# Second attention: ScalarE's copies of minus the maxima also for five odd full tiles of each head

## The reference

```python
x = x + attn_a(layernorm(x))      # 16 heads of 64, full softmax, own norm behind it
x = x + ffn(layernorm(x))         # 128 -> 512 -> 128, relu
x = x + attn_b(layernorm(x))      # 8 heads of 128, rope, causal
x = x + ffn(layernorm(x))

def attn_b(x):                    # called the second attention below
    q, k, v = x @ w_aq, x @ w_ak, x @ w_av          # per head, 128 wide
    q, k = rope(q), rope(k)
    s = einsum('ihd,jhd->hij', q, k) / 128
    s = s - 1e30 * (i < j)                          # causal
    p = softmax(s)
    return (p @ v) @ w_ao
```

## Time and profile before

| what | value |
|---|---|
| median of 3 runs | 1911.57 us (1911.49 to 1912.69) |
| the profiled execution, its own time | 1914.15 us |
| span of its profile | 1912.3 us |
| PE busy in the span | 1838.2 us (96%) |
| ACT busy | 1620.6 us (84%) |
| POOL busy | 1596.8 us (84%) |
| DVE busy | 1458.4 us (76%) |
| exponentials of even tiles, copies L938 | 160 |
| seeds L942 | 159 |

### The profile page before, as it was taken

One profiled execution on the slowest core, in us unless ns is written; L12 is line 12 of the kernel. 1 busy time (PEld: TensorE's weight loads), 2 busy tenths in 40 slices (PEclk: granted clock), 3 DMA queues, 4 the chain that ended last, 5 costly groups with the idle time before them and its releaser, 6 DMA issues.

```text
span 1912.3 us, 56624 instructions
## 1 busy us (share of the span) xinstructions
PE 1838.2 (96%) x23763; PEld 1259.8 (66%) x23763; DVE 1458.4 (76%) x2679; ACT 1620.6 (85%) x2080; POOL 1596.8 (84%) x1022
## 2 busy tenths in 40 slices
PE   4899999999999999999999999779999999999998
PEld 3566666666666666666666666447777777777766
DVE  7798878878878878878878875567777778777752
ACT  4799999999999999999999999648787787887884
POOL 2899999999999999999999999448787787887852
PEclk8999999999999999999999999789999999999999
DMA  4201101100100100100100100100000000000000
GB/s 117 67 11 27 35 12 25 35 13 24 35 15 22 35 17 21 35 16 22 35 19 19 35 2 2 56 1 2 2 2 2 2 2 2 2 2 2 2 2 23
DMA packets 45038, 38.01 MB, mean 20 GB/s; under 512 B 8304, under 2 KB 44144, under 8 KB 44528
## 3 DMA queue, kind: packets, MB, share of 16 engines
q1 hardware_dynamic: 44544, 34.19, 7.1%
q10 hardware_dynamic: 240, 0.20, 0.0%
HBM read 8.15 MB, written 1.05 MB: 5 GB/s over the span
## 4 chain that ended last, share of the span: by engine, by line
PE 78%; POOL 8%; DVE 5%; issue 5%; ACT 4%; DMA 0%; SPq 0%; POOLq 0%; ACTq 0%; DVEq 0%
PE ST L1684 11%; PE ST L1685 11%; PE RING L1555 7%; PE OO L1646 6%; PE OO L1648 6%; PE OO L1645 6%; POOL PBUF L711 6%; PE OO L1555 4%; PE ST L1749 2%; PE ST L1882 2%; PE OO L1770 2%; PE ST L1884 1%; PE ST L1883 1%; PE OO L1904 1%; PE OO L1906 1%
## 5 line engine op out<-in xcount | busy, mean ns | idle before, releaser
L627 POOL TENSOR_TENSOR PAB<-PR,PAB 128x1024 f16<-128x1024 f32 x342 | 724.2, 2133 | 42.1 <-ACT PAB L814 40.1
L814 ACT ACTIVATE PAB<-ST,exp_scale 128x1024 f16<-128x1024 f32 x512 | 569.1, 1112 | 0.0
L1139 DVE TENSOR_REDUCE maxes<-RING 128x1 f32<-128x512 f32 x661 | 440.3, 685 | 122.6 <-PE RING L1555 118.1
L1645 PE MATMUL OO<-VP,PAB 128*128 128x66 f16 x4096 | 446.6, 192 | 2.9 <-POOL PAB L627 2.9
L1646 PE MATMUL OO<-VP,PAB 128*128 128x64 f16 x4096 | 447.1, 193 | 0.0
L1648 PE MATMUL OO<-VP,PAB 128*128 128x66 f16 x4096 | 445.2, 192 | 0.0
L812 ACT ACTIVATE PR<-ST,exp_scale 128x1024 f32<-128x1024 f32 x342 | 382.7, 1119 | 66.3 <-PE ST L1685 64.1
L1645 PEld LDWEIGHTS OO<-VP,PAB 128*128 128x128 f16 x4096 | 380.3, 96 | 78.3 <-issue 15.6
L1646 PEld LDWEIGHTS OO<-VP,PAB 128*128 128x128 f16 x4096 | 377.0, 97 | 60.7
L1684 PE MATMUL ST<-QL,KH 128*128 128x512 f16 x1024 | 389.1, 380 | 2.1 <-DVE QH L1151 1.0
L1685 PE MATMUL ST<-QH,KL 128*128 128x512 f16 x1024 | 389.1, 380 | 0.0
(11 more groups left out here) (320 smaller groups left out, 4159.3 us busy)
## 6 DMA issues: line engine op xcount, KB each, us to landing
KH<-HS SPq DMA_DIRECT2D x126, 64.0 KB, 2.0
QL<-HS SPq DMA_DIRECT2D x64, 64.0 KB, 2.0
QL<-LS SPq DMA_DIRECT2D x64, 64.0 KB, 2.0
QH<-HS SPq DMA_DIRECT2D x64, 64.0 KB, 2.0
KL<-LS SPq DMA_DIRECT2D x63, 64.0 KB, 2.0
X<-in_L_attn_a_x SPq DMA_DIRECT2D x4, 256.0 KB, 3.9
SHARED<-in_rope_cos SPq DMA_DIRECT2D x1, 1024.0 KB, 4.9
SHARED<-in_rope_sin SPq DMA_DIRECT2D x1, 1024.0 KB, 7.3
```

Of the source, the lines that this page charges most:

```text
L627: pool.tensor_tensor(PB[:, s, :], PRA[g % PR_SLOTS], PA[:, s, :], ALU.subtract).then_inc(p_low_ready, 1)
L814: act.activation(PA[:, step % SLOTS_A, :], ST[step % 2][:, :], ACT.Exp, scale=scale).then_inc(sa.exps, 1)
L1139: dve.reduce_max(maxes[:, i // BLOCKS, i % BLOCKS:i % BLOCKS + 1], bank[:, :], X_AXIS).then_inc(sa.ring_taken, 1)
L1645: pe.matmul(o, high, v[:, 0:V2_AT], start=(m == 0 and qt == 0), stop=False, skip_group_check=True)
```

## The change

The table `SEEDED_TOO` names five places of a head: (2, 3), (2, 7), (3, 3), (3, 7) and (3, 11). All are odd and full tiles. `seeded(t)` is true for every even tile but 0, as before, and for these. For a seeded tile t, ACT treats tile t - 2 as it treated even tiles before: one exponential from the bank, the high part as a copy from SBUF, and then the seed of tile t. PE leaves out the four spread matmuls of t and waits for the seed. The semaphores `first_exps` and `seeds` now count by `SEEDED_COUNT`. The five tiles of t - 2 are (2, 1), (2, 5), (3, 1), (3, 5) and (3, 9). Over 8 heads 40 tiles change.

```diff
+SEEDED_TOO = {(2, 3), (2, 7), (3, 3), (3, 7), (3, 11)}
+def seeded(t):
+    it, ul, step = PLACES_B[t]
+    return t > 0 and (t % 2 == 0 or (ul % BLOCKS, step) in SEEDED_TOO)
+SEEDED_COUNT = np.cumsum([seeded(t) for t in range(len(PLACES_B))]).tolist()
...
-                if g % 2:
-                    act.activation(p, SB[1][:, c0:BLK], ACT.Exp, scale=scale)
+                if g + 2 < len(PLACES_B) and seeded(g + 2):
+                    act.activation(p, SB[g % 2][:, c0:BLK], ACT.Exp, scale=scale).then_inc(sbb.first_exps, 1)
                     wait(act, sbb.pv, g - SLOTS_B + 1)
-                    act.activation(PAH[:, g % SLOTS_B, c0:BLK], SB[1][:, c0:BLK], ACT.Exp, scale=scale
+                    act.wait_ge(sbb.first_exps, seeded_up_to(g + 2))
+                    act.activation(PAH[:, g % SLOTS_B, c0:BLK], p, ACT.Copy).then_inc(sbb.exps, 1)
+                    tile, seed, taken = seed_of(g + 2)
+                    act.wait_ge(sbb.ring_taken, taken)
+                    act.activation(tile, seed, ACT.Copy).then_inc(sbb.seeds, 1)
+                else:
+                    act.activation(p, SB[g % 2][:, c0:BLK], ACT.Exp, scale=scale)
+                    wait(act, sbb.pv, g - SLOTS_B + 1)
+                    act.activation(PAH[:, g % SLOTS_B, c0:BLK], SB[g % 2][:, c0:BLK], ACT.Exp, scale=scale
                                    ).then_inc(sbb.exps, 1)
...
-                if g % 2 or g == 0:
+                if not seeded(g):
                     wait(pe, sbb.exps, g - 1)
                     spread(SB[g % 2], qb, max(0, step - BT * qb))
                 else:
-                    pe.wait_ge(sbb.seeds, g // 2)
+                    pe.wait_ge(sbb.seeds, seeded_up_to(g))
```

More of the change, by code:

```diff
@@ L251, with seeded_up_to @@
 ITEMS_B, ROWS_OF_B, VALUES_OF_B, END_B = number_items_b()
+SEEDED_TOO = {(2, 3), (2, 7), (3, 3), (3, 7), (3, 11)}
+def seeded(t):
+    it, ul, step = PLACES_B[t]
+    return t > 0 and (t % 2 == 0 or (ul % BLOCKS, step) in SEEDED_TOO)
+def seeded_up_to(t):
+    return SEEDED_COUNT[t]
+SEEDED_COUNT = np.cumsum([seeded(t) for t in range(len(PLACES_B))]).tolist()
 def output_of_last_head_b(block):
@@ L928, in _ @@
                 p = PRB[g % PR_SLOTS_B][:, c0:BLK]
-                if g % 2:
-                    act.activation(p, SB[1][:, c0:BLK], ACT.Exp, scale=scale)
+                if g + 2 < len(PLACES_B) and seeded(g + 2):
+                    act.activation(p, SB[g % 2][:, c0:BLK], ACT.Exp, scale=scale).then_inc(sbb.first_exps, 1)
                     wait(act, sbb.pv, g - SLOTS_B + 1)
-                    act.activation(PAH[:, g % SLOTS_B, c0:BLK], SB[1][:, c0:BLK], ACT.Exp, scale=scale
-                                   ).then_inc(sbb.exps, 1)
[L934 to L942, removed]
+                    act.wait_ge(sbb.first_exps, seeded_up_to(g + 2))
[7 more added lines that the diff above has]
+                    act.activation(PAH[:, g % SLOTS_B, c0:BLK], SB[g % 2][:, c0:BLK], ACT.Exp, scale=scale
+                                   ).then_inc(sbb.exps, 1)
                 for n, item in ITEMS_B[g]:
```

## The result

| | before | after |
|---|---|---|
| median | 1911.57 us (5 runs, 1910.77 to 1912.69) | 1919.02 us (5 runs, 1917.45 to 1919.42) |
| ratio | | 1.003, 95% interval 1.002 to 1.0041 |
| profiled execution, its own time | 1914.15 us | 1919.02 us |
| span of the profile | 1912.3 us | 1917.2 us |
| first scores of the second attention to its last | 597.05 us | 603.03 us |

The change makes the kernel slower by 0.3%: 5.7 us by the ratio, 7.4 us between the two medians. The forecast was 1916.8 us, +5.3; the measured median lies 2.2 us above it, at the upper edge of the forecast's own range of 1915 to 1919. The two profiled executions differ by 4.9 us in span, and by 6.0 between the first and the last scores of the second attention: the one before began them 1.1 us later (1275.14 against 1274.03 us), which the change cannot have done.

A forecast was written before the change was run, and what follows sets the result against it. PE is busiest, but ACT's queue sets PE's start at (2, 4). Six heads at +0.64, head 6 +0.42 and the last head +1.0 sum to +5.3 us: 1916.8 us, own range 1915 to 1919, stated range 1910.5 to 1923.

The forecast's parts named there:

- What bounds: Second attention: PE is busiest, 8.8 us of matmuls leave it, but ACT's queue sets PE's start at (2, 4).
- (2, 3): Third unit: ACT's queue makes the scores of (2, 4) 0.70 us late.
- (2, 7): Third unit: PE's 0.22 us saving is lost to POOL before (2, 8), shift +0.71; head 6 keeps the 0.22.
- (3, 3), (3, 7), (3, 11): Fourth unit, running shift: +0.32 after (3, 3), +0.15 after (3, 8), -0.07 after (3, 11).
- The last head: Third unit 0; fourth unit bound by ACT, 2.10 us added against 1.1 of gaps, +1.0 us.
- The sum: Whole kernel: 6 x 0.64 + 0.42 + 1.0 = +5.3 us, median 1916.8 us.
- The signs in the profile: Wait at (2, 4) about 0.8 us, third unit 22.5, ACT busy some 26 more, PE idle about 14 more.
- A: Whole kernel: seeds hide everywhere and PE gives its time back, -8.8 us, 1902.8 us; chance 0.09.
- B: Loss at (2, 4) is made up later; a head costs 0 to +0.4, 1911.6 to 1915.4 us; chance 0.27.
- C: ACT becomes the bound at all five places, 0.48 us each, 40 times, +19 us, 1931; chance 0.08.

The follow-up runs named there:

- The copy at (2, 1): Kernel before with one more 128x512 ACT copy behind the exponentials of (2, 1), no seed added; third unit 22.26 or 22.27 us in heads 0 to 5.
- The two late places alone: Kernel before plus seeds at (3, 7) and (3, 11) only, not in the last head; ratio 0.9987 of before, median 1910.14 us.
- The kernel with the 12 matmuls: The whole change plus 12 matmuls no result uses, in PE's wait before the scores of (3, 6) in the last head; ratio 1.0019 of before.

## Why the prediction was right

**What bounds.** Right. PE was the busiest, and taking 8.8 us of matmuls from it made the kernel slower, because ACT's queue set PE's start at one tile in each head.

**(2, 3).** Forecast: scores of (2, 4) 0.70 late. Measured: 0.65. The price was a little high: a changed tile holds ACT 1.81 us here (1456.44 to 1458.25), not 1.84, and tile (2, 2) behind it 1.82 (1458.77 to 1460.59); in both the copy starts 0.76 us after the exponential, where it was 0.78 before. Why is not shown. The copy at (2, 1) shows the mechanism with nothing else changed.

**(2, 7).** Right: nothing gained in heads 0 to 5, by POOL's hold on the values of (2, 8). In head 6 the forecast kept 0.22 and had its third unit at +0.49; measured +0.43 (22.35 against 21.92). That they lie so near is luck: (2, 7) saved 0.51 there, by DVE's seed row as well, and the delay of 0.28 made up for it.

**(3, 3), (3, 7), (3, 11).** Forecast -0.07 for the fourth unit, measured -0.09. The two late places alone gave 0.37 of 0.44, so (3, 3) costs 0.28 if the places add up, against the 0.32 of the forecast.

**The last head.** The third unit came out at -0.08, forecast 0. In the fourth ACT was the bound as said; its price was 0.82 instead of 1.0. What the forecast had not in it is the granted clock: the execution profiled after the change had the drop, the one before had not, which adds 29.96 - 28.39 = 1.57 us to the difference of the two profiles. The wait around which it comes is the same in both kernels, 2.93 us and 2.92.

**The sum.** 6 x 0.56 (0.65 - 0.09) + 0.33 (0.43 - 0.10) + 0.74 (0.82 - 0.08) = 4.4 us by the units, where the forecast had 5.3. The 0.28 of head 6 is in it; without that it is 4.2. With the clock's 1.57 and the 0.28 of head 4 it makes 6.3, less about 0.3 from the first two units of the heads: the 6.0 of the two profiles. The kernel with the 12 matmuls, whose clock did not fall, takes 601.50 us from the first scores to the last, 4.4 more than before. The ratio's 5.7 us (3.8 to 7.8) holds both the forecast and, within its lower part, the 4.4. So the mechanism held place by place and the prices were a little too high; that 5.3 came nearer to the ratio's 5.7 than the 4.4 of the parts is luck. The 1.3 us between 4.4 and 5.7 is within the interval, and these times do not tell what it is made of.

**The signs in the profile.** The wait at (2, 4) was to be 0.8 us and is 0.66. ACT was to be busy 26 us more; it is 17.8 (1638.4 against 1620.6), in part since ACT stands still for 0.09 us between a changed tile's exponential and its copy (1457.11 to 1457.20), 3.6 us over 40 tiles; the rest of the difference is not traced. PE's idle time was to grow by about 14 us and grew by 10.3 (from 74.1 to 84.4).

**The rivals.** A, everything hidden: out, PE waits more, not less. B, the loss made up later: out in heads 0 to 5, where 0.65 late at (2, 4) is 0.66 at the end of the unit; in head 6 it came true, 0.51 of the 0.65 comes back. (By its own terms B's lower end was 1912.6 us, not 1911.6.) C, ACT the bound at all places: holds in the last head's fourth unit only; in the others (2, 3) and (3, 3) cost, and (3, 7) and (3, 11) gain.

## What to carry to other kernels

An engine's busy share does not say whether work may be moved to it; the gap after the very instruction does. Before moving work, look at the place where the busiest engine waits for the other one, follow that queue back to its last gap, and add only behind that gap: here the same 0.5 us of ACT cost 0.50 at one tile and nothing four tiles on, and two places with slack gave 0.13% where five gave a loss. A saving that lies ahead of another engine's hold is lost in that hold.

A number that fits may do so by two errors: head 6 was met within 0.06 us by a gain of 0.51, of which the forecast had 0.22, and a delay of 0.28, which it had not.

## What was not expected of the hardware

Around the end of a wait of about 2.9 us in an otherwise dense stream, TensorE's granted clock fell to its lower level for some 3.4 us (nearly 7 in one) in eight of the eleven profiled executions. That cost 1.4 to 2.7 us each where the unit was otherwise as before. It did so in neither of the two in which 12 matmuls filled 2.75 us of that wait. It came and went between kernels that are alike in this unit, so one profile of each is not enough to compare them by some 2 us. What decides in which execution it falls is open.

The same goes for the start of the second attention, which the change does not touch. The first unit of head 0 lasts 11.94 to 11.97 us in the six profiles in which the clock is low in it for 3.4 us, and 13.65 to 14.40 in the seven in which it is low for 6.3 to 10.4 us (14.40 before, 14.31 after). So times from the first scores to the last are compared only between profiles alike in this unit, as those above of the kernels before, after, and with the 12 matmuls are.

VectorE's instruction of 128x4 elements (L1127) takes 0.23 us by itself, and up to 1.20 us behind a POOL instruction. In the kernel before, a POOL instruction is under way at its start in 30 of 32 cases of the second attention. In all 30 POOL's instruction ends first, in 29 of them by 0.02 to 0.03 us; the longest, 1.18 to 1.20 us, are those that start 0.10 or 0.11 us behind POOL's. In head 6 a shift of 0.21 us between the two queues made 1.06 us into 0.23, and that took away a wait of PE.
